# Last layer's second quantised product: Pool rounds the lower four channel blocks, VectorE the upper four

## The chip, the cores and the metric

The kernel runs on one core of one Trainium2 chip. The time is the device time of the whole program in microseconds (us), median of the runs. The core's engines are TensorE (PE in the profile, its weight loads PEld), VectorE (DVE), ScalarE (ACT), GpSimd (POOL, here called Pool) and SyncE (SP). They run side by side, each works through its own queue in order, and they meet only at semaphores: an instruction that waits holds back everything behind it on its engine.

## The reference, cut to what matters

The input is x of shape (4, 1024, 256). Four layers follow one another, each an attention over a context of 77 rows and a feed-forward part. The change is in the feed-forward part of the last layer:

```python
def act_quant(x):
    scale = 127.0 / jnp.clip(jnp.max(jnp.abs(x), axis=-1, keepdims=True), 1e-05)
    return jnp.clip(jnp.round(x * scale), -128, 127) / scale
def weight_quant(w):
    scale = 1.0 / jnp.clip(jnp.mean(jnp.abs(w)), 1e-05)
    return jnp.clip(jnp.round(w * scale), -1, 1) / scale
def bit_linear(x, w):
    return jnp.einsum('bsd,hd->bsh', act_quant(x), weight_quant(w))  # straight-through term left out
h = bit_linear(x, w1)                      # 256 -> 1024 channels
h = depthwise_conv1d(h, conv_w, conv_b)    # width 3, along the tokens
h = jax.nn.silu(h)
return bit_linear(h, w2)                   # 1024 -> 256 channels
```

For the second product each token has its own scale, 127 over the largest absolute value among its 1024 channels. So no value can be scaled and rounded before all 1024 channels of that token are there.

## The kernel before, in words

`layer_3` (from L2377) works on one batch b of 1024 tokens after another, four in all (B = 4). A batch is two groups g of 512 tokens (G = 2, TOK = 512), a group four tiles of 128 tokens (TT = 4). Each batch has an attention part of eight units (`attention_dve`, `attention_act`, `attention_pool`, `attention_pe`), in which VectorE subtracts the row maximum from the scores, ScalarE takes the exponential, VectorE sums, Pool multiplies by the reciprocal sum (L286), and TensorE transposes and multiplies; after it the first product, the convolution and SiLU.

The hidden values of a batch lie in SBUF as `SL`, 128 partitions x 8 channel blocks (NHC = 8, HALF = 4) x 1024 tokens in f32, channels on the partitions. TensorE turns each block (L2586), VectorE takes the maxima (L2747). When all eight are done, VectorE works out 127 / maximum (L2753 to L2757), TensorE spreads it over the partitions (L2632), and ScalarE copies it to SBUF as `S2B` (L2542; the tile bears the name L3PT in the profile). Then comes what is called the tail here, four VectorE instructions for each group, each over 4 blocks x 512 tokens, that is 128 x 2048 elements:

- L2762 multiplies the lower four blocks of `SL` by the scale, in place; both of its inputs are in SBUF.
- L2763 does so for the upper four, and is linked: VectorE waits for its end.
- L2764 rounds the lower four into `SQ` (bf16), by adding and subtracting a large constant (MAGIC); one input, in SBUF.
- L2765 rounds the upper four, and raises `q_ready[g]`.

The order is group 0 entirely, then group 1. `second_product` (L2559 on, its products are L2566) waits for `q_ready[g]` and runs 32 products of 128 x 256, the eight blocks of one token tile after another. For batches 0 to 2 it is called within the attention of the next batch: TensorE's queue has the scores of unit 0 and of unit 1 for both groups ahead of `second_product(0)`, those of unit 2 ahead of `second_product(1)`. For the last batch both stand at the end of the program, followed by `add_output` on VectorE (L2697) and the stores. On VectorE the next batch's attention stands directly behind the tail; its first instructions are L245 (maximum over scores in PSUM) and L246 (subtraction, one input in PSUM, one in SBUF). On Pool, whose queue in this layer holds the attention's L286, the bias L2467 and the next batch's keys and values (`last_layer_context`, L2084 and L2086), nothing stands between those keys and values and the first L286 of the next batch.

Of the kernel before, what the change touches and what calls it, by code (L numbers as in the profile page):

```python
# [10 lines left out]
ALU = mybir.AluOpType  # L11
# [10 lines left out]
G = 2  # L22
TT = 4
TOK = TT * P
# [10 lines left out]
MAGIC = 12582912.0  # L35
# [111 lines left out]
def bc_last(ap, n):  # L147

    return ap.unsqueeze(len(ap.shape)).to_broadcast(list(ap.shape) + [n])


def bc_at(ap, axis, n):
    v = ap.unsqueeze(axis)
    shape = list(v.shape)
    shape[axis] = n
    return v.to_broadcast(shape)
# [1924 lines left out]
def last_layer_context(eng, L, headof, blockhead):  # L2081

    for c in range(KC):
        eng.tensor_tensor(L["Kbd"][c][:, :, :], bc_at(L["ctxT3"][:, c, :], 1, HH), bc_last(headof[:, :], CTXP), ALU.mult)  # L2084
    for j in range(BLK):
        last = eng.tensor_tensor(L["Vbd"][j][:, :, :].rearrange("p c (h d) -> p c h d", d=DH),  # L2086
                                 L["ctxrows"][:, j, :].rearrange("p (c h d) -> p c h d", c=KC, d=DH),
                                 bc_at(bc_last(blockhead[:, j, :], DH), 1, KC), ALU.mult)
    return last
# [287 lines left out]
def layer_3(L, nc, a, sbt, GP, SC, ident, identb, onesf, headof, blockhead, eps, tokno, spare, x1rows, buf, out):  # L2377
    ctx = ExitStack()
    BT = G * TT
    HALF = NHC // 2  # L2380
    with ctx:
        def sb(name, shape, dt=f32):
            return sbt(name, shape, dt, ctx)
# [18 lines left out]
        SL = sb("SL", [P, NHC, S])  # L2402
        SQ = sb("SQ", [P, NHC, S], bf16)

        S2B = T["PT"][1][:, :, :, :].rearrange("p a b c -> p (a b c)")[:, 0:S]
# [8 lines left out]
        with rnd:  # L2414
            sa = Sems(nc, rnd)
            sm = {n: sa.pair("l3_" + n) for n in ATTENTION_SEMS + (
                "x_in", "x_out", "var1_ready", "sd1_ready", "rstd1_ready", "xn1_ready",
                "var2_ready", "sd2_ready", "rstd2_ready", "xn2_ready", "xt_psum", "xt_ready",
                "y_psum", "y_taken", "xqt_psum", "sx_ready", "xr_ready", "xq_ready", "xq_high", "xq_low", "h_psum", "z0_ready", "z_ready", "s_ready",
                "am_ready", "tile_psum", "tile_taken", "s2_psum", "s2_ready", "q_ready", "o_psum", "o_ready",  # L2420
                "x_bias")}
            vchain, ctx_in, kv_ready = (sa.one("l3_" + n) for n in ("vchain", "ctx_in", "kv_ready"))

            with nc.Block() as block:
# [35 lines left out]
                @block.gpsimd  # L2460
                def _(pool):
                    for b in range(B):
                        def after_unit(v):
                            if v < G:
                                x = X[b % 2][v][:, :, :]
                                pool.wait_ge(sm["xn1_ready"][v], b + 1)
                                nc.gpsimd.tensor_tensor(x, x, bc_at(bo3r[:, :], 1, TT), ALU.add).then_inc(sm["x_bias"][v], 1)  # L2467
                        attention_pool(nc, pool, T, sm, b, after_unit)
                        if b + 1 < B:
                            for g in range(G):  # L2470
                                pool.wait_ge(sm["ot_psum"][g], UNITS * (b + 1))
                            pool.wait_ge(ctx_in, CTX_IN * (b + 1))
                            last_layer_context(nc.gpsimd, L, headof, blockhead).then_inc(kv_ready, 1)

                @block.scalar
                def _(act):
# [71 lines left out]
                def _(pe):  # L2548
# [12 lines left out]

                    def second_product(g, b):
                        pe.wait_ge(sm["q_ready"][g], b + 1)
                        for t in range(TT):
                            for h in range(NHC):
                                last = nc.tensor.matmul(GP[g][:, t * D:(t + 1) * D], SQ[:, h, (g * TT + t) * P:(g * TT + t + 1) * P], w2q[:, h, :],  # L2566
                                                        start=h == 0, stop=h == NHC - 1)
                        last.then_inc(sm["o_psum"][g], 1)
# [73 lines left out]
                def _(dve):  # L2642
                    link = Chain(dve, vchain)
                    tt, tsc, stt = nc.vector.tensor_tensor, nc.vector.tensor_scalar, nc.vector.scalar_tensor_tensor
# [62 lines left out]
                    for b in range(B):  # L2707
                        def after_slot(slot):
                            if b and 0 < slot <= G:
                                add_output(slot - 1, b - 1)  # L2710
                        attention_dve(nc, dve, T, sm, b, link, SC, after_slot)
                        for g in range(G):
                            add_projection(g, b, 0)
                        for g in range(G):
                            add_projection(g, b, 1)
                        for g in range(G):
                            ln_rstd(g, b, 2)
                        if b + 1 < B:
                            tokens_stats(0, b + 1)
                        for g in range(G):  # L2720
                            quantise(g, b)
                        if b + 1 < B:
                            tokens_stats(1, b + 1)
                        for g in range(G):
                            dve.wait_ge(sm["xr_ready"][g], b + 1)
                            for t in range(TT):
                                xn = T["XN"][g][:, t, :]
                                last = tsc(xn, xn, MAGIC, isx[g][:, t:t + 1], ALU.subtract, ALU.mult)
                            last.then_inc(sm["xq_ready"][g], 1)
                        if b + 1 < B:  # L2730
                            for g in range(G):
                                ln_rstd(g, b + 1, 1)
                        for g in range(G):
                            dve.wait_ge(sm["xq_high"][g], b + 1)
                            hi, lo = (v[:, :, :].rearrange("p k n -> p (k n)") for v in XQ[g])
                            tt(lo, GP[g][:, :], hi.bitcast(f32), ALU.subtract).then_inc(sm["xq_low"][g], 1)

                        for h in range(NHC + 2):
                            if h < NHC:
                                z, y = Z[h % 2], SC[h % 2]  # L2740
                                dve.wait_ge(sm["z0_ready"][h % 2], b * HALF + h // 2 + 1)
                                link(stt(z[:, 1:S], y[:, 0:S - 1], cwc[:, h, 0:1], z[:, 1:S], ALU.mult, ALU.add))  # L2742
                                stt(z[:, 0:S - 1], y[:, 1:S], cwc[:, h, 2:3], z[:, 0:S - 1], ALU.mult, ALU.add).then_inc(sm["z_ready"][h % 2], 1)  # L2743
                            if h >= 2:
                                i = h - 2
                                dve.wait_ge(sm["tile_psum"][i % 2], b * HALF + i // 2 + 1)
                                nc.vector.tensor_reduce(amh[:, :, i], GP[i % 2][:, :].rearrange("p (t n) -> p t n", n=P), AX, ALU.max,  # L2747
                                                        apply_absolute_value=True).then_inc(sm["tile_taken"][i % 2], 1)
                        for i in range(2):
                            dve.wait_ge(sm["tile_taken"][i], (b + 1) * HALF)  # L2750
                        for g in range(G):
                            s = slice(g * TT, (g + 1) * TT)
                            link(nc.vector.reduce_max(am2[:, s], amh[:, s, :], AX))  # L2753
                            link(tsc(am2[:, s], am2[:, s], 1e-5, None, ALU.max))
                            link(nc.vector.reciprocal(s2[:, s], am2[:, s]))
                            tsc(s2[:, s], s2[:, s], 127.0, None, ALU.mult).then_inc(sm["am_ready"][g], 1)
                            link(tsc(os2[:, s], am2[:, s], 1.0 / 127.0, wm2[:, :], ALU.mult, ALU.mult))  # L2757
                        for g in range(G):
                            tok = slice(g * TOK, (g + 1) * TOK)
                            low, high, by = SL[:, 0:HALF, tok], SL[:, HALF:, tok], bc_at(S2B[:, tok], 1, HALF)  # L2760
                            dve.wait_ge(sm["s2_ready"][g], b + 1)
                            tt(low, low, by, ALU.mult)  # L2762
                            link(tt(high, high, by, ALU.mult))  # L2763
                            tsc(SQ[:, 0:HALF, tok], low, MAGIC, MAGIC, ALU.add, ALU.subtract)  # L2764
                            tsc(SQ[:, HALF:, tok], high, MAGIC, MAGIC, ALU.add, ALU.subtract).then_inc(sm["q_ready"][g], 1)  # L2765
                    for g in range(G):
                        add_output(g, B - 1)
# [51 lines left out]
```

## Time and profile before

| | us |
|---|---|
| median of 3 runs | 2816.32 (2815.0 to 2820.91) |
| the profiled execution | 2818.34 |
| its span, first to last instruction | 2816.6 |
| PE / DVE / ACT / POOL busy in the span | 2333.1 / 1941.5 / 1471.4 / 1035.7 |
| layer 3's four tails, first L2762 of each | starts at 2407.03, 2536.86, 2666.64, 2793.21 |

Busy time is summed over the whole program, so it doesn't say what a stage waits for. The timeline gives, in order of time, the instructions of each engine with their start, the time they took (equal neighbours are merged, with their count), and in brackets how long the engine had been idle before and what ended that. The chain of waits follows the work that ended last back through what released it. The granted clock (PEclk) is TensorE's clock as a share of 2.4 GHz: 0.50 is the lower level, 1.2 GHz, and 1.00 the upper.

### The profile page before, as it was taken

To read this page: it belongs to the slowest core of one execution; us is meant where nothing else is said; L and a number is where in the kernel's file an instruction comes from. 1 tells how busy PE (TensorE), PEld (TensorE's weight loads), DVE (VectorE), ACT (ScalarE), POOL (GpSimd) and SP (SyncE) were. 2 spreads that over 40 slices of the span, in tenths; PEclk is the share of its full clock that TensorE was granted. 3 is DMA by queue.
4 is the path that set the end of the run, shared out by engine and by line. 5 is a ranking of instruction groups with operands and counts; after the bars stand their busy time and mean duration, and the time that the engine had idled before them with its cause. 6 is when DMAs were issued, how large, how long until landed. Compare 5 with 4: busy or idle time off the path is not lost. (4 is left out here: it accounts for less than half of the span.)

```text
span 2816.6 us, 43303 instructions
## 1 busy us (share of the span) xinstructions
PE 2333.1 (83%) x16184; PEld 1911.5 (68%) x16184; DVE 1941.5 (69%) x4456; ACT 1471.4 (52%) x2446; POOL 1035.7 (37%) x1011
## 2 busy tenths in 40 slices
PE   4778888877589999999975999999999956767575
PEld 2445455554377888888865999999999935445444
DVE  4698888895355666666654666676666647978877
ACT  2457777664355565565452544444455435454543
POOL 3243444432132344443453444454444432213030
PEclk9789988886789999999987999999999978888887
DMA  8600000000100001100014555555555320001000
GB/s 266 229 1 17 4 14 16 8 9 8 33 16 1 26 28 44 48 31 21 17 50 142 112 126 141 137 116 134 141 133 130 65 52 11 31 11 31 0 16 15
DMA packets 144472, 171.03 MB, mean 61 GB/s; under 512 B 16920, under 2 KB 114053, under 8 KB 144264
## 3 DMA queue, kind: packets, MB, share of 16 engines
q1 hardware_dynamic: 114360, 136.15, 14.7%
q0 software_dynamic: 29184, 31.99, 7.8%
q8 instruction: 129, 2.11, 0.3%
q14 instruction: 79, 0.65, 0.1%
q10 hardware_dynamic: 720, 0.12, 0.0%
HBM read 100.73 MB, written 74.32 MB: 62 GB/s over the span
## 5 line engine op out<-in xcount | busy, mean ns | idle before, releaser
L2191 POOL DMA_INDIRECT x_after_l<-rowsout,target x160 | 266.6, 1666 | 319.6 <-DVE rowsout L2317 261.5
L162 PE MATMUL SC<-Xhi,Whi 128*128 128x320 f32 x1024 | 321.7, 314 | 6.6 <-DVE HF L2359 3.6
L162 PE MATMUL SC<-Xhi,Wlo 128*128 128x320 f32 x1024 | 317.5, 310 | 0.0
L162 PE MATMUL SC<-Xlo,Whi 128*128 128x320 f32 x1024 | 317.3, 310 | 0.0
L645 POOL TENSOR_TENSOR PR<-PR,rs 128x616 f32<-128x616 f32 x128 | 163.2, 1275 | 390.4 <-DVE rs L1039 390.4
L1406 POOL TENSOR_TENSOR ff_Hlo<-ff_HF,ff_Hhi 128x512 fp32r<-128x512 f32 x108 | 143.2, 1326 | 387.8 <-ACT ff_Hhi L1539 387.8
L2288 ACT ACTIVATE SG<-SC 128x320 f32<-128x320 f32 x256 | 111.9, 437 | 237.3 <-PE SC L162 235.9
L2324 DVE TENSOR_TENSOR Hlo<-HF,Hhi 128x320 fp32r<-128x320 f32 x256 | 129.7, 507 | 104.3 <-ACT Hhi L2276 104.3
L162 PEld LDWEIGHTS SC<-Xhi,Whi 128*128 128x128 f32 x1024 | 193.4, 189 | 10.1 <-DVE HF L2359 7.2
L1808 DVE TENSOR_TENSOR ff_HF<-ff_HG,SC 128x512 f32<-128x512 f32 x112 | 76.7, 685 | 172.6 <-ACT ff_HG L1533 112.9
L162 PEld LDWEIGHTS SC<-Xlo,Whi 128*128 128x128 f32 x1024 | 193.5, 189 | 0.0
L162 PEld LDWEIGHTS SC<-Xhi,Wlo 128*128 128x128 f32 x1024 | 193.2, 189 | 0.0
L286 POOL TENSOR_TENSOR L3PR<-L3PR,L3rs 128x616 f32<-128x616 f32 x64 | 76.9, 1226 | 315.4 <-DVE L3rs L253 315.2
L2276 ACT ACTIVATE Hhi<-HF 128x320 fp32r<-128x320 f32 x256 | 120.7, 472 | 130.9 <-DVE HF L2359 130.8
L162 PE MATMUL GP<-Whi,Hhi 128*128 128x256 f32 x640 | 182.6, 285 | 4.9 <-DVE Hlo L2324 2.8
L162 PE MATMUL GP<-Wlo,Hhi 128*128 128x256 f32 x640 | 182.5, 285 | 0.0
L162 PE MATMUL GP<-Whi,Hlo 128*128 128x256 f32 x640 | 182.3, 285 | 0.0
L181 PE MATMUL SC<-Kbd,QT 64*128 64x308 f32 x512 | 120.5, 552 | 52.7 <-DVE PR L1033 48.8
L744 ACT ACTIVATE PT<-GP 128x640 f32<-128x640 f32 x128 | 89.6, 700 | 116.4 <-PE GP L895 115.9
L2359 DVE TENSOR_TENSOR HF<-SG,SC 128x320 f32<-128x320 f32 x256 | 124.1, 485 | 34.2 <-ACT SG L2288 32.7
L895 PE MATMUL GP<-ident,PR 128*128 128x128 f32 x640 | 111.9, 314 | 42.5 <-ACT OT L740 25.8
L1419 POOL DMA_INDIRECT expert_in<-raw,ff_slot_in x128 | 127.7, 998 | 50.3 <-issue 33.5
(498 smaller groups left out, 6874.4 us busy)
## 6 DMA issues: line engine op xcount, KB each, us to landing
expert_in<-zeros SPq DMA_DIRECT2D x4, 5440.0 KB, 35.7
rowsin<-expert_in SPq DMA_DIRECT2D x32, 680.0 KB, 4.5
first_expert<-L_wg SPq DMA_DIRECT2D x16, 512.0 KB, 5.4
first_expert<-L_wu SPq DMA_DIRECT2D x16, 512.0 KB, 6.4
first_expert<-L_wd SPq DMA_DIRECT2D x16, 512.0 KB, 7.4
Wraw<-L_wg SPq DMA_DIRECT2D x16, 512.0 KB, 5.5
Wraw<-L_wu SPq DMA_DIRECT2D x16, 512.0 KB, 6.4
Wraw<-L_wd SPq DMA_DIRECT2D x16, 512.0 KB, 7.3
```

The costliest lines, as they stand in the source:

```text
L162: last = nc.tensor.matmul(out, lhs[l], rhs[r], start=start and n == 0, stop=stop and n == 2)
L181: last = nc.tensor.matmul(o[j], q[r], K[r, 4 * j:4 * j + 4, 0:CTX], start=mask is None, stop=True)
L645: nc.gpsimd.tensor_tensor(pr, pr, bc_last(rs[n % NPA][:, :], CTX), mult).then_inc(pnorm, 1)
L744: nc.scalar.activation(PT[:, n % 2, :, :], ptrans[:, 0:BLK * P].rearrange("p (k n) -> p k n", n=P), ACT.Copy).then_inc(pt_ready, 1)
L895: last = nc.tensor.transpose(ptrans[:, k * P:(k + 1) * P], pr[:, k * P:(k + 1) * P], ident[:, :])
L1406: nc.gpsimd.tensor_tensor(lo[:, :], HF[q % 2][:, :], hi[:, :].bitcast(f32), ALU.subtract).then_inc(h_low, 1)
L1419: nc.gpsimd.indirect_dma_start(buf[:, :], bass.IndirectOffsetOnAxis(ap=slot_in[g][:, t, k:k + 1], axis=0), T["XS"][g][:, t, :], None, boun ...
L2191: nc.gpsimd.indirect_dma_start(x1rows[:, :], bass.IndirectOffsetOnAxis(ap=target[j % 2][:, t:t + 1], axis=0), rowsout[j % 2][:, t, :], Non ...
L2276: nc.scalar.activation(Hsp[q // NU % 2][0][:, h, n * CC:(n + 1) * CC], HF[q % 2][:, :], ACT.Copy).then_inc(h_high, 1)
L2288: nc.scalar.activation(SG[u % 2][:, :], SC[u % 2][:, 0:CC], ACT.Silu).then_inc(s_ready, 1)
L2324: nc.vector.tensor_tensor(lo_, HF[q % 2][:, :], hi_.bitcast(f32), ALU.subtract).then_inc(h_made, 1)
L2359: nc.vector.tensor_tensor(HF[u % 2][:, :], SG[u % 2][:, :], SC[u % 2][:, 512:512 + CC], ALU.mult).then_inc(h_mult, 1)
```

## The change

Pool takes over the rounding of the lower four blocks (128 x 2048, f32 to bf16) for both groups. VectorE multiplies the lower blocks of both groups first, each raising a new semaphore `scaled[g]`; then it multiplies and rounds the upper blocks group by group. Pool raises `low_rounded[g]`, and `second_product` waits for it beside `q_ready[g]`. Pool's two instructions stand behind the next batch's keys and values in its queue.

```diff
@@ gpsimd, end of each batch
                             last_layer_context(nc.gpsimd, L, headof, blockhead).then_inc(kv_ready, 1)
+                        for g in range(G):
+                            tok = slice(g * TOK, (g + 1) * TOK)
+                            pool.wait_ge(sm["scaled"][g], b + 1)
+                            nc.gpsimd.tensor_scalar(SQ[:, 0:HALF, tok], SL[:, 0:HALF, tok], MAGIC, MAGIC, ALU.add, ALU.subtract)\
+                                .then_inc(sm["low_rounded"][g], 1)
@@ tensor
                     def second_product(g, b):
                         pe.wait_ge(sm["q_ready"][g], b + 1)
+                        pe.wait_ge(sm["low_rounded"][g], b + 1)
@@ vector, the tail
                         for g in range(G):
                             tok = slice(g * TOK, (g + 1) * TOK)
-                            low, high, by = SL[:, 0:HALF, tok], SL[:, HALF:, tok], bc_at(S2B[:, tok], 1, HALF)
+                            low = SL[:, 0:HALF, tok]
                             dve.wait_ge(sm["s2_ready"][g], b + 1)
-                            tt(low, low, by, ALU.mult)
-                            link(tt(high, high, by, ALU.mult))
-                            tsc(SQ[:, 0:HALF, tok], low, MAGIC, MAGIC, ALU.add, ALU.subtract)
+                            tt(low, low, bc_at(S2B[:, tok], 1, HALF), ALU.mult).then_inc(sm["scaled"][g], 1)
+                        for g in range(G):
+                            tok = slice(g * TOK, (g + 1) * TOK)
+                            high = SL[:, HALF:, tok]
+                            link(tt(high, high, bc_at(S2B[:, tok], 1, HALF), ALU.mult))
                             tsc(SQ[:, HALF:, tok], high, MAGIC, MAGIC, ALU.add, ALU.subtract).then_inc(sm["q_ready"][g], 1)
```

## Rows read from the trace of the kernel before

**Rows 1.** Chain of waits, 2400 to 2432 us (start, us, what).
```profile
2406.33 0.60 ACT L3PT L2542
...
2420.72 0.72 DVE L3mx L245
...
2422.32 0.70 PE SC L178 x2
```
**Rows 2.** Timeline around the first tail (start, us, engine, line, operation, idle before).
```profile
2407.03 2.29 DVE L2762 TENSOR_TENSOR SL<-SL,L3PT 128x2048 f32<-128x2048 f32 x1 [0.80 <-ACT L3PT L2542]
...
2420.64 0.79 DVE L245 TENSOR_REDUCE L3mx<-SC 128x8 f32<-128x616 f32 x1
...
2426.25 3.71 PE L2566 MATMUL GP<-w2q,SQ 128*128 128x256 bf16 x32
...
2429.01 2.40 POOL L286 TENSOR_TENSOR L3PR<-L3PR,L3rs 128x616 f32<-128x616 f32 x2 [75.62 <-DVE L3rs L253]
```
**Rows 3.** Timeline of DVE alone, the last tail.
```profile
2793.21 2.29 DVE L2762 TENSOR_TENSOR SL<-SL,L3PT 128x2048 f32<-128x2048 f32 x1 [0.80 <-ACT L3PT L2542]
2795.42 2.28 DVE L2763 TENSOR_TENSOR SL<-SL,L3PT 128x2048 f32<-128x2048 f32 x1
2797.74 1.23 DVE L2764 TENSOR_SCALAR SQ<-SL 128x2048 bf16<-128x2048 f32 x1
2798.88 1.22 DVE L2765 TENSOR_SCALAR SQ<-SL 128x2048 bf16<-128x2048 f32 x1
2800.01 2.28 DVE L2762 TENSOR_TENSOR SL<-SL,L3PT 128x2048 f32<-128x2048 f32 x1
...
2804.53 1.23 DVE L2764 TENSOR_SCALAR SQ<-SL 128x2048 bf16<-128x2048 f32 x1
2805.68 1.22 DVE L2765 TENSOR_SCALAR SQ<-SL 128x2048 bf16<-128x2048 f32 x1
2806.81 1.65 DVE L2697 SCALAR_TENSOR_TENSOR X<-GP,os,X 128x256 f32<-128x256 f32 x4
```
**Rows 4.** Timeline of PE alone, the last second products.
```profile
2800.15 6.14 PE L2566 MATMUL GP<-w2q,SQ 128*128 128x256 bf16 x32 [6.71 <-DVE SQ L2765]
2806.95 3.67 PE L2566 MATMUL GP<-w2q,SQ 128*128 128x256 bf16 x32 [0.65 <-DVE SQ L2765]
```
**Rows 5.** Busy time by window (window, length, PE to POOL busy, PEclk, DMA).
```profile
2800.10:2803.00 2.90, 2.85 (x14) 2.04 (x15) 2.90 (x2) 0.00 (x0) 0.00 (x0) 0.50 0.00 0
```
**Rows 6.** Timelines of DVE and of POOL, one DVE instruction without and with Pool.
```profile
870.82 0.48 DVE L1869 TENSOR_TENSOR ff_PR<-ff_PR,ff_rs 128x308 f32<-128x308 f32 x1
...
953.21 1.47 DVE L1869 TENSOR_TENSOR ff_PR<-ff_PR,ff_rs 128x308 f32<-128x308 f32 x1
...
953.05 1.29 POOL L1406 TENSOR_TENSOR ff_Hlo<-ff_HF,ff_Hhi 128x512 fp32r<-128x512 f32 x1 [5.70 <-ACT ff_Hhi L1539]
```
**Rows 7.** Timelines of DVE and of POOL, 1087.0 to 1089.8 us.
```profile
1087.13 1.23 DVE L1969 TENSOR_TENSOR ff_XTlo<-ff_XT,ff_XThi 128x1024 fp32r<-128x1024 f32 x1 [0.20 <-ACT ff_XThi L1485]
...
1087.63 1.87 POOL L1406 TENSOR_TENSOR ff_Hlo<-ff_HF,ff_Hhi 128x512 fp32r<-128x512 f32 x1 [0.70 <-ACT ff_Hhi L1539]
```
**Rows 8.** Timelines of DVE and of POOL, two DVE instructions back to back.
```profile
1521.26 2.36 DVE L2302 TENSOR_TENSOR Wlo<-first_expert,Whi 128x1024 fp32r<-128x1024 f32 x2 [13.20 <-ACT Whi L2264]
...
2080.47 2.37 DVE L2302 TENSOR_TENSOR Wlo<-Wraw,Whi 128x1024 fp32r<-128x1024 f32 x2 [0.46 <-ACT Whi L2264]
...
2080.56 1.19 POOL L2180 TENSOR_TENSOR mine<-mine 128x10 f32<-128x10 f32 x1
```
**Rows 9.** Groups of Pool's instructions, whole span (count, busy us, mean ns, idle before).
```profile
L2180 POOL TENSOR_TENSOR mine<-mine 128x10 f32<-128x10 f32 x32 | 8.3, 260 | 2.5
L485 POOL TENSOR_SCALAR_AFFINE_SELECT spread<-spread 80x640 f32<-80x640 f32 x8 | 6.0, 747 | 1.1
L1425 POOL TENSOR_TENSOR ff_wd_lo<-raw,ff_wd_hi 128x2560 fp32r<-128x2560 f32 x1 | 5.6, 5640 | 31.1 <-ACT ff_wd_hi L1543 31.1
...
L485 POOL TENSOR_SCALAR_AFFINE_SELECT ident<-ident 128x128 f32<-128x128 f32 x1 | 0.3, 287 | 0.2 <-POOL spread L490 0.2
```

More of the change, by code:

```diff
@@ L2419, in layer_3 @@
                 "y_psum", "y_taken", "xqt_psum", "sx_ready", "xr_ready", "xq_ready", "xq_high", "xq_low", "h_psum", "z0_ready", "z_ready", "s_ready",
-                "am_ready", "tile_psum", "tile_taken", "s2_psum", "s2_ready", "q_ready", "o_psum", "o_ready",
+                "am_ready", "scaled", "low_rounded", "tile_psum", "tile_taken", "s2_psum", "s2_ready", "q_ready", "o_psum", "o_ready",
                 "x_bias")}
```

## The prediction

> **What bounds the kernel now.** I read the chain of waits first, around a tail in the middle of the layer. ScalarE's copy of the scale ends it from the one side, then VectorE's eight tail instructions follow without a break, then the next batch's first maximum L245, and only then TensorE's next scores, L178 [rows 1]. So in batches 0 to 2 the tail is on the path whole: from the start of L2762 at 2407.03 to the start of L245 at 2420.64 are 13.61 us [rows 2], and the reader is to see that L245 has no idle time before it. What the tail loses or gains, the next attention starts sooner or later. Two things have slack there. The second product of group 0 starts only at 2426.25, 19.2 us after the tail began, and Pool's next own work at 2429.01, after 75.62 us of idleness [rows 2].
>
> The last batch is another case, since nothing follows but the second products. The timeline of VectorE gives the steps from one start to the next [rows 3]: L2762 to L2763 2.21 us, L2763 to L2764 2.32 (the link costs 0.1), L2764 to L2765 1.14, L2765 to the next 1.13; together 13.60 for both groups. Group 0's `q_ready` comes 6.9 us after the tail's start, and TensorE begins at 2800.15, at a granted clock of 0.50, the level of 1.2 GHz [rows 4, 5], after 6.71 us of idleness. Its 32 products take 6.14 us. Group 1's begin at 2806.95, 13.74 after the tail's start, and take 3.67 [rows 4]. Between the two TensorE is idle for 0.65. That number decides much below: only 0.65 us can group 0 come later before the end moves.
>
> **The change part by part.** Counted from the start of a tail, with no disturbance by Pool, VectorE's queue after the change would be: L2762 for group 0 at 0, for group 1 at 2.21, upper product of group 0 at 4.42, its rounding at 6.74, upper product of group 1 at 7.88, its rounding at 10.20, next work at 11.33. Removed are two roundings, 2 x 1.14 = 2.28 us. Group 0's `q_ready` would be at 6.74 + 1.22 = 7.96, so 1.07 later than before, because it now has three products ahead of it and not two.
>
> Pool gets two roundings of 128 x 2048. The trace has no large one-input Pool instruction with a bf16 result. The nearest is L485, one input: 747 ns for 640 elements, 287 for 128 [rows 9], so 0.90 ns an element, and 287 + 1920 x 0.90 = 2.01 us for 2048. The other end is Pool with two full inputs, L1425: 5640 ns for 2560 elements, 2.20 ns each, so 4.5 us. Nothing speaks for a rounding below 2.0. I take 2.01, since the instruction has one input, and keep 4.5 for the range.
>
> Now whether Pool's work lies beside VectorE's. A VectorE product of two SBUF tiles, L1869, takes 0.48 us alone; where Pool's L1406 had begun 0.16 earlier it takes 1.47 [rows 6]. So it did not share, it stood still 0.99 us, to 0.14 before Pool's record ends. The other direction: L1406, 1.29 us in [rows 6], takes 1.87 where it begins 0.50 after VectorE's L1969, another product of two SBUF tiles [rows 7]. Its end at 1089.50 lies 1.14 after L1969's end; it did next to nothing in between. These are exclusive turns. All of VectorE's multiplications in the tail have two SBUF inputs. Pool's rounding reads SBUF as L1406 does. I expect that nothing overlaps: each of Pool's roundings takes its 2.01 - 0.14 = 1.87 us out of VectorE's time, where it falls between VectorE's SBUF instructions. The rounding on VectorE, 1.14 us a step for 2048 elements, nearly two elements in a ns, is the form that I expect to be excluded too, though that is argued from the two-input rows.
>
> The Trainium skill, page "SBUF — State Buffer", section "Who interferes with whom", says the same of both kinds: VectorE with two SBUF inputs, or in a two-port mode, and a GpSimd instruction that reads SBUF take the shared ports for a whole instruction in turn, and whoever comes second stands still. Rows 6 and 7 agree for two inputs, with 0.99 us and 0.58 us; by this rule the forecast below stands, and without it the second rival does. Its page "GPSIMD Engine Reference", section "Engine selection", calls one-input work on GpSimd roughly line rate, which with its 1.2 GHz would be an estimate of 1.7 us for 2048 elements, 0.3 under my term; the sum would be some 2 us smaller.
>
> Next, who goes first. `scaled[0]` comes at 2.29, when the second L2762 has begun (2.21). Pool stands waiting until that ends at 4.42. Does Pool get in there, though VectorE's next instruction is queued without a gap? One place shows it: Pool's L2180 began 0.09 us after the first of two back-to-back L2302, and ended at 2081.75, just behind the first (half of the pair's 2.37 lies at 2081.66) and far ahead of the second's end at 2082.84 [rows 8]. It took 1.19 where it has a mean of 0.26 [rows 9]. The VectorE pair took 2.37 in place of 2.36 [rows 8], so it gave way only as long as those 10 elements need. Whoever waits comes next. So Pool rounds group 0 at 4.42 to 6.3, ahead of the upper product of group 0. Whether its second rounding follows at once or after that product makes no difference: in both orders it is ahead of the rounding of the upper blocks of group 0.
>
> The middle batches: 11.33 + 2 x 1.87 = 15.07 in place of 13.60, that is 1.47 later each, and three of them 4.4 us. `low_rounded[0]` comes by 6.5 and `low_rounded[1]` by 10.6, far ahead of TensorE's 19.2, so the new wait on TensorE costs nothing; behind it stand the scores of unit 2. If that cover were gone, each us would hold back TensorE, and with it those scores. Pool's own attention work is not moved, it has 8 us between L245 and L286 [rows 2].
>
> The last batch: `q_ready[0]` at 7.96 + 3.74 = 11.70, 4.8 later than before. TensorE starts at 11.75 cold as before and needs 6.14, to 17.89; `q_ready[1]` at 15.2 is earlier than that, so group 1 follows at once, to 21.56. Before it ended at 13.74 + 3.67 = 17.41. That is 4.15 us later, which is more than the VectorE time, since TensorE's slow product is now the path. The last add and the stores follow unchanged.
>
> The sum is 4.4 + 4.15 = 8.5 us more. Of the profiled execution's 2818.34 that makes 2826.9; the median of the runs is 2.02 lower, 2816.32, and I predict it as 2824.8. Within this case the turns may fall otherwise: if Pool's second rounding were to come only after group 0's upper rounding, group 0 would be ready 1.87 sooner and the sum 6.7. With 0.3 us more or less for a rounding it moves by 4 tails x 2 x 0.3 = 2.4. The likeliest case has its own range at 2822 to 2828.
>
> **The rivals.**
>
> First, the same turns with a slow Pool. At 4.5 us a rounding, 4.36 of it in VectorE's way, a middle tail is 11.33 + 8.72 = 20.05, 6.45 more, three 19.4. The last has `q_ready[0]` at 16.68, TensorE's end at 16.7 + 6.14 + 3.67 = 26.5, 9.1 later. Sum 28.5, 2844.8. For it speaks the conversion to bf16 with two operations in one instruction, which L485 doesn't show. Against it, that L1425's price is that of two inputs.
>
> Second, on the other side: no exclusion, because Pool's one-input reading and VectorE's products do lie beside each other. Then each middle tail gains 2.28, three 6.8. In the last TensorE starts at 8.0 and ends at 8.0 + 6.14 + 3.67 = 17.8, 0.4 later than before. Sum -6.4, 2809.9. The point from which a middle tail gains is at 1.14 us of VectorE's time for each of Pool's roundings, half of the 2.28 removed. Against it stand rows 6 and 7; for it, that both show Pool with two inputs.
>
> Third, Pool finds no gap and gets through only behind VectorE's last rounding, at 11.33. The middle tails gain 2.28 each all the same, as L245 and L246 read PSUM and TensorE's 19.2 is not reached by 15.3. In the last, `low_rounded[0]` comes at 13.3, TensorE ends at 13.4 + 6.14 + 3.67 = 23.2, 5.8 later. Sum -6.8 + 5.8 = -1.0, 2815.3. Against it stands the one place in rows 8, for it that this is one place only, with 10 elements.
>
> **How the numbers follow.** A measurement of this kernel can tell a difference of about 0.2%, 5.6 us. The forecast has a chance of 0.55, the slow Pool 0.15, no exclusion 0.10, Pool behind VectorE 0.15, and 0.05 are for what I don't see. The range goes from 2813 to 2844: below are most of the second rival and a part of the unseen, above nearly half of the first. Faster by over 0.2% is the second rival in its better half and little else, 0.08. Within 0.2% are the third, the rest of the second, and 0.05 of the forecast with a quicker Pool, 0.24. Slower is what remains, 0.68.
>
> **What would show it.** In the changed kernel's timeline the middle tail from the first L2762 to the next L245 should be near 15.1 us. One or two VectorE instructions of the tail should show durations of 4 us or so in place of 2.28 or 1.22, each ending where a Pool rounding ends plus its own length. Pool's first rounding should begin at 2.4 and seem long, since it stands waiting from there to 4.4. Group 0's last products should begin near 11.8 us. The prediction is wrong if the six VectorE instructions that are left in a tail keep their durations (then the second or third rival, told apart by Pool's durations), or if the middle tails are above 17 us (the first).

## The result and the profile after

The changed kernel takes 2843.82 us (median of 4 runs, 2842.74 to 2845.12), the kernel before 2816.68 beside it: ratio 1.0097, 95% interval 1.0083 to 1.0111, 27.1 us slower. The forecast was 8.5 us slower. Direction and place were right, the size is off by a factor of three, and the time stands near the price of the first rival (28.5 us slower).

The first middle tail after the change, timelines of VectorE and of Pool (start, us, engine, line, operation, idle before); it answers to [rows 2, 3].

```profile
2404.93 4.49 DVE L2768 TENSOR_TENSOR SL<-SL,L3PT 128x2048 f32<-128x2048 f32 x2 [0.81 <-ACT L3PT L2547]
2409.34 6.60 DVE L2772 TENSOR_TENSOR SL<-SL,L3PT 128x2048 f32<-128x2048 f32 x1
2415.98 1.50 DVE L2773 TENSOR_SCALAR SQ<-SL 128x2048 bf16<-128x2048 f32 x1
2417.40 6.57 DVE L2772 TENSOR_TENSOR SL<-SL,L3PT 128x2048 f32<-128x2048 f32 x1
2424.01 1.49 DVE L2773 TENSOR_SCALAR SQ<-SL 128x2048 bf16<-128x2048 f32 x1
2425.42 0.78 DVE L245 TENSOR_REDUCE L3mx<-SC 128x8 f32<-128x616 f32 x1
...
2407.31 9.09 POOL L2477 TENSOR_SCALAR SQ<-SL 128x2048 bf16<-128x2048 f32 x1 [56.02 <-DVE SL L2768]
2416.39 8.03 POOL L2477 TENSOR_SCALAR SQ<-SL 128x2048 bf16<-128x2048 f32 x1
```

The reader is to see three things. The tail takes 2425.42 - 2404.93 = 20.49 us in place of 13.61. Both lower products keep their length, 4.49 for two; each upper product takes 6.6 in place of 2.28, that is 4.3 more, and each upper rounding 1.5 in place of 1.22. And Pool's two roundings are recorded from 2407.31 to 2424.42 without a gap, with waiting in both: the first stands until the second lower product ends at 2409.42, and the second, 8.03 us long, begins while VectorE's rounding of group 0 (2415.98 to 2417.48) is still going on.

The last second products, timeline of TensorE, which answers to [rows 4]:

```profile
2824.02 5.04 PE L2572 MATMUL GP<-w2q,SQ 128*128 128x256 bf16 x32 [12.34 <-DVE SQ L2773]
2832.04 3.67 PE L2572 MATMUL GP<-w2q,SQ 128*128 128x256 bf16 x32 [2.98 <-DVE SQ L2773]
```

The last tail starts at 2811.45, so group 1's products start 20.59 us behind it, where it was 13.74. The loss adds up from four equal parts: from the first to the last tail the changed kernel takes 2811.45 - 2404.93 = 406.52 us, before 386.18, so 20.3 for three tails; in the last one 6.85. That is 27.2. Where TensorE's slow product was to be the path in the last batch, it is not: it is idle for 2.98 us between the groups.

### The profile page after: what moved, and what is told of

The parts are those of the page before. It is cut to its first block and busy times, and to the rows that moved or that the text cites. A ratio compares the mean times of both kernels' runs of the same rounds, so it can differ in the third digit from the quotient of the medians.

```text
span 2841.7 us, 43311 instructions
## 1 busy us (share of the span) xinstructions
PE 2329.0 (82%) x16184; PEld 1910.0 (67%) x16184; DVE 1969.2 (69%) x4448; ACT 1471.1 (52%) x2446; POOL 1103.9 (39%) x1019
## 5 line engine op out<-in xcount | busy, mean ns | idle before, releaser
L2477 POOL TENSOR_SCALAR SQ<-SL 128x2048 bf16<-128x2048 f32 x8 | 68.3, 8551 | 235.1 <-DVE SL L2768 235.1
```

## The experiments

### Is Pool slow by itself, or are both slowed by being together?

The first theory, T: Pool's rounding is simply long, and VectorE waits for a part of it. The rival, R: Pool alone needs the 2.0 us of the forecast, and the two slow each other.

```diff
                             high = SL[:, HALF:, tok]
+                            for i in range(G):
+                                dve.wait_ge(sm["low_rounded"][i], b + 1)
                             link(tt(high, high, bc_at(S2B[:, tok], 1, HALF), ALU.mult))
```

> VectorE waits for both of Pool's roundings before the upper products, so that Pool and VectorE never read SBUF side by side after the lower products. In the changed kernel Pool's first rounding ended 6.98 us after the second lower product; take away the 2.28 us of VectorE's product that lay in it and 4.70 are left. Theory T (turns, and Pool is slow by itself): alone Pool still needs about 4.7 us a rounding, VectorE's L2772 and L2773 fall back to 2.28 and 1.22, and a middle tail is 4.5 + 2 x 4.7 + 6.9 = 20.8 us, where the changed kernel has 20.5; the time is 2844 to 2850. Rival R (each slows the other, Pool alone would be the 2.0 us of the forecast): Pool 2.0 a rounding, tail 4.5 + 4.0 + 6.9 = 15.4 us, 5.1 less each, time near 2825.

Measured: 2862.78 us, ratio to before 1.0158 (1.0141 to 1.0175), above the range of either. The timelines of Pool and of VectorE in this run:

```profile
2410.47 16.15 POOL L2477 TENSOR_SCALAR SQ<-SL 128x2048 bf16<-128x2048 f32 x2 [56.02 <-DVE SL L2768]
...
2426.73 2.29 DVE L2774 TENSOR_TENSOR SL<-SL,L3PT 128x2048 f32<-128x2048 f32 x1 [14.14 <-POOL SQ L2477]
2429.06 1.23 DVE L2775 TENSOR_SCALAR SQ<-SL 128x2048 bf16<-128x2048 f32 x1
```

With Pool alone, VectorE's instructions are back at 2.29 and 1.23. But Pool is not at 4.7: from the end of the second lower product (2412.58) to Pool's end (2426.62) are 14.0 us, 7.0 a rounding. The view of the line (minimum, median, maximum in ns) has the second rounding, which waits for nothing, as the minimum:

```profile
L2477 POOL TENSOR_SCALAR SQ<-SL x8: 7075/8066/9095, 2410.5 to 2837.3; 128x2048 bf16<-128x2048 f32 x8
```

R is refuted. T is right in kind and wrong in number: I had subtracted VectorE's 2.28 us from Pool's 6.98, as if they had excluded each other. They had overlapped, which is why this kernel, where they can't, is 19 us slower still than the changed one.

### What a Pool instruction costs by its form

Eight Pool instructions were added to the kernel before, each once in each of the batches 0 to 2. Shown are only they, with remarks; the scratch tiles are left out (`src` and `dstb` have rows of 512, `fsrc`, `fdstb` and `fdst` are contiguous, a `b` at the end means bf16).

```diff
+plink(nc.gpsimd.tensor_scalar(dstb, src, MAGIC, MAGIC, ALU.add, ALU.subtract))     # rows of 512, bf16
+plink(nc.gpsimd.tensor_scalar(fdstb, fsrc, MAGIC, MAGIC, ALU.add, ALU.subtract))   # contiguous, bf16
+plink(nc.gpsimd.tensor_scalar(fdst, fsrc, MAGIC, MAGIC, ALU.add, ALU.subtract))    # contiguous, f32
+plink(nc.gpsimd.tensor_scalar(fdstb, fsrc, MAGIC, None, ALU.add))
+plink(nc.gpsimd.tensor_scalar(fdst, fsrc, MAGIC, None, ALU.add))
+plink(nc.gpsimd.tensor_tensor(fdst, fsrc, fsrc, ALU.mult))
+plink(nc.gpsimd.tensor_copy(fdst, fsrc))
+plink(nc.gpsimd.tensor_scalar(fdstb[:, 0:TOK], fsrc[:, 0:TOK], MAGIC, MAGIC, ALU.add, ALU.subtract))
```

> The kernel before, with eight more Pool instructions per batch in Pool's idle stretch before the tail, each 128 x 2048 (the last 128 x 512) on scratch tiles, one after the other: the changed kernel's form (four rows of 512, f32 to bf16, add and subtract), the same contiguous, the same with f32 output, with one operation and bf16, with one operation and f32, a product of two inputs, a copy, and the first form on 512 elements. It leaves nothing out. Theory T: the first form takes 4.7 to 4.9 us with nobody beside it. Rival R: 2.0 us. If T, the rows say what costs: bf16 output, the second operation, or the rows; I expect the second operation and the conversion to share the 2.7 us above 2.0, contiguity nothing. The time should be that of before, Pool having slack there.

Measured: 2900.42 us, one execution. The timeline of Pool in this run, eight forms in the order of the diff:

```profile
2507.71 7.09 POOL L2480 TENSOR_SCALAR pc<-pa 128x2048 bf16<-128x2048 f32 x1
2514.88 7.09 POOL L2481 TENSOR_SCALAR pc<-pa 128x2048 bf16<-128x2048 f32 x1
2522.05 7.08 POOL L2482 TENSOR_SCALAR pb<-pa 128x2048 f32<-128x2048 f32 x1
2529.22 5.37 POOL L2483 TENSOR_SCALAR pc<-pa 128x2048 bf16<-128x2048 f32 x1
2534.67 5.36 POOL L2484 TENSOR_SCALAR pb<-pa 128x2048 f32<-128x2048 f32 x1
2540.11 3.60 POOL L2485 TENSOR_TENSOR pb<-pa 128x2048 f32<-128x2048 f32 x1
2543.78 1.89 POOL L2486 COPY pb<-pa 128x2048 f32<-128x2048 f32 x1
2545.76 2.01 POOL L2487 TENSOR_SCALAR pc<-pa 128x512 bf16<-128x512 f32 x1
```

Rows and bf16 cost nothing, though I had given the conversion a share. The second operation costs 1.72 us. The form itself costs most: with one operation it takes 5.36, nearly three times the copy's 1.89, and more than a product (3.60, here of a tile with itself). From 512 to 2048 elements it rises by 5.08, 3.3 ns an element. So a one-input Pool instruction can be slower than a two-input one, and my upper end of 4.5 us was no upper end.

The trace of before had a better hint, in rows I had passed over. Groups of Pool's instructions in the kernel before, the same form on small tiles with one operation (count, busy us, mean ns):

```profile
L2178 POOL TENSOR_SCALAR mine<-rowsin 128x20 f32<-128x20 f32 x32 | 9.3, 292 | 73.0 <-DMA x_after_l<-rowsout,target 69.4 <-DMA rowsin<-expert_in 3.6
...
L2182 POOL TENSOR_SCALAR empty<-rowsin 128x5 f32<-128x5 f32 x32 | 7.8, 243 | 2.8
```

49 ns for 15 elements are 3.3 ns each, which for 2048 makes 6.9 us. These rows have one operation, for which it is too much (5.4), so that it comes near the 7.1 of two operations is in part luck; L485, which I took, is another operation and gave 2.0.

I had expected the time of before, since Pool is idle in this stretch. It was 83 us more, because VectorE was delayed there, as is told below.

### Held, or served in turn?

How can VectorE's product lose 4.3 us beside an instruction of 7.1, and both end within 0.5 us of each other? The run with the forms has an instruction that tells it, a VectorE one of 4 elements with two SBUF inputs, begun 0.08 us behind Pool's first form. Timelines of VectorE and of Pool:

```profile
2350.29 4.45 DVE L2691 SCALAR_TENSOR_TENSOR L3nw<-L3nw,L3rstd 128x4 f32<-128x4 f32 x1
2354.78 0.16 DVE L2692 SCALAR_TENSOR_TENSOR L3rstd<-L3nw,L3rstd 128x4 f32<-128x4 f32 x1
...
2350.21 7.12 POOL L2480 TENSOR_SCALAR pc<-pa 128x2048 bf16<-128x2048 f32 x1
```

It stood still for 4.3 us, the next of the same kind took 0.16 again, though Pool's instruction went on until 2357.33. So VectorE and Pool meet not only at semaphores, but also where both read SBUF. To see the same in the tail, the upper product was cut in two.

```diff
-                            link(tt(high, high, bc_at(S2B[:, tok], 1, HALF), ALU.mult))
+                            for k in range(2):
+                                part = high[:, k * 2:(k + 1) * 2, :]
+                                last = tt(part, part, bc_at(S2B[:, tok], 1, 2), ALU.mult)
+                            link(last)
```

> The upper product of each group is cut in two of 128 x 1024, with no wait between them. Two readings of the 6.57 us that an upper product takes beside Pool's 7.08 us rounding. Held (theory H): VectorE stands still for about 4.3 us, as L2691 on 4 elements did in the run with Pool's forms (4.45 us in place of 0.16), and then runs at full speed beside the rest of Pool's instruction: first half 4.3 + 1.2 = 5.5 us, second half 1.2. Paced (rival P): both instructions get an element in turn, 3.2 ns each: two halves of about 3.3 us. The time is 2844 in both.

Measured: 2843.43 us, 1.0094 (1.0076 to 1.0113). The two halves of the first upper product in VectorE's timeline, and the view of the line:

```profile
2409.77 5.54 DVE L2774 TENSOR_TENSOR SL<-SL,L3PT 128x1024 f32<-128x1024 f32 x1
2415.23 1.21 DVE L2774 TENSOR_TENSOR SL<-SL,L3PT 128x1024 f32<-128x1024 f32 x1
...
L2774 DVE TENSOR_TENSOR SL<-SL,L3PT x16: 1209/3356/5539, 2409.8 to 2829.8; 128x1024 f32<-128x1024 f32 x16
```

The first half takes 5.54 and the second 1.21, in group 1 likewise 5.50 and 1.21. The median of 3356 ns lies halfway between the two kinds and is no instruction's own length. Held it is: VectorE stands for 4.3 us, then runs at full speed beside the rest of Pool's instruction. Why Pool lets go of reading there is not shown.

### Is it the second SBUF input?

The changed kernel, with the scale read from PSUM. The diff is cut to what matters; VectorE waits for TensorE (`s2_psum`) where it waited for ScalarE's copy.

```diff
-                            tt(low, low, bc_at(S2B[:, tok], 1, HALF), ALU.mult)
+                            tt(low, low, bc_at(SC[g][:, 0:TOK], 1, HALF), ALU.mult)
-                            link(tt(high, high, bc_at(S2B[:, tok], 1, HALF), ALU.mult))
+                            link(tt(high, high, bc_at(SC[g][:, 0:TOK], 1, HALF), ALU.mult))
-                            nc.scalar.activation(S2B[...], SC[g][:, 0:TOK], ACT.Copy)
+                                pe.wait_ge(sm["q_ready"][g], b)     # ahead of the next batch's first scores
```

> The scale is read by VectorE from PSUM, where TensorE wrote it, so that the four products of a tail have only one SBUF input; ScalarE's copy (0.60 us) falls away, and the next batch's scores wait for q_ready. Theory T with the exclusion tied to VectorE's second SBUF input: all products keep about 2.3 us though Pool is at work beside them; only L2773-like roundings still wait for Pool. The tail is between 12 us (one short wait) and 17 us (both Pool roundings ahead of the first upper rounding), the time 2810 to 2828. Rival R (whatever reads SBUF on VectorE is slowed by Pool): products stay near 6.6 us, tail near 20 us, time about 2840.

Measured: 2830.39 us, 1.0044 (1.0027 to 1.0060), a little above the range given. Timelines of VectorE and Pool:

```profile
2409.38 2.28 DVE L2771 TENSOR_TENSOR SL<-SL,SC 128x2048 f32<-128x2048 f32 x1
2411.70 3.87 DVE L2772 TENSOR_SCALAR SQ<-SL 128x2048 bf16<-128x2048 f32 x1
2415.48 2.27 DVE L2771 TENSOR_TENSOR SL<-SL,SC 128x2048 f32<-128x2048 f32 x1
2417.79 5.79 DVE L2772 TENSOR_SCALAR SQ<-SL 128x2048 bf16<-128x2048 f32 x1
2423.50 0.78 DVE L245 TENSOR_REDUCE L3mx<-SC 128x8 f32<-128x616 f32 x1
...
2407.36 15.14 POOL L2477 TENSOR_SCALAR SQ<-SL 128x2048 bf16<-128x2048 f32 x2 [55.39 <-DVE SL L2767]
```

The products are at 2.28 with Pool at work beside them: it is the second SBUF input that makes them wait. Now the roundings wait. The second ends at 2423.58, 1.08 behind Pool's end at 2422.50, so it did nothing until Pool was through. That is the other kind of conflict: VectorE's rounding, nearly two elements in a ns, stands until the end of Pool's instruction. The first one shows it best: it begins at 2411.70, 4.34 us after Pool's, about when a product would have been let go, and ends only at 2415.57. The tail is 18.5 us and not 12 to 17, because Pool's instruction was longer than I then believed.

It also explains the 83 us of the run with the forms, most of them at least: its first tail starts 24.8 us later than that of before, and the next two stretches from tail to tail are 28.9 and 27.9 longer. VectorE's small one-input instructions ahead of the feed-forward part's first product are of this second kind. L2702, L2704 and L2742 take 28.2 us there in the first batch, in the kernel before 2.8. L2704, 4 elements, took 6.92 us and ended with Pool's instruction:

```profile
2364.77 6.92 DVE L2704 TENSOR_SCALAR sx<-sx 128x4 f32<-128x4 f32 x1
...
2364.59 7.08 POOL L2482 TENSOR_SCALAR pb<-pa 128x2048 f32<-128x2048 f32 x1
```

The Trainium skill, page "SBUF — State Buffer", section "Summary: rules for kernel authors", has both kinds, and says that the second one to issue stands until the first is through. For the fast rounding the runs agree. For two SBUF inputs they differ: 4.3 us of 7.1.

### The order alone

VectorE does all four roundings again, in the changed kernel's order; Pool's part and its semaphores, taken out, are not shown.

```diff
                             link(tt(high, high, bc_at(S2B[:, tok], 1, HALF), ALU.mult))
+                            tsc(SQ[:, 0:HALF, tok], SL[:, 0:HALF, tok], MAGIC, MAGIC, ALU.add, ALU.subtract)
                             tsc(SQ[:, HALF:, tok], high, MAGIC, MAGIC, ALU.add, ALU.subtract)
```

> The changed kernel's order on VectorE (both lower products first) with all four roundings on VectorE and none on Pool. T: middle tails 13.6 us as before; in the last batch group 0 is ready 2.2 us later, of which 0.65 were slack, so 1.5 us in all, about 2818. If the order itself carried a part of the 27 us loss, it would show here as more than 3 us.

Measured: 2816.61 us, 0.9997 (0.9988 to 1.0007). So the order carries at most 2.0 of the 27.1 us. The 1.5 us expected would lie within the interval; the timeline shows that they didn't come. The last products of this run, all 64 in one row of TensorE's timeline:

```profile
2799.12 8.61 PE L2566 MATMUL GP<-w2q,SQ 128*128 128x256 bf16 x64 [8.91 <-DVE SQ L2768]
```

They start 9.14 us behind the tail's start, as worked out, but end 17.75 behind it, only 0.34 later than before. My 6.14 us for group 0 hung on where in them the granted clock rose and was no property of the work: before, it stood at 0.50 for 4.9 us from their start; in the changed kernel, where the same 32 products took 5.04, it was at 1.00 again 3 us after it.

### The forecast's own case: a short Pool instruction

```diff
-                            nc.gpsimd.tensor_scalar(SQ[:, 0:HALF, tok], SL[:, 0:HALF, tok], MAGIC, MAGIC, ALU.add, ALU.subtract)
+                            nc.gpsimd.tensor_copy(SQ[:, 0:HALF, tok], SL[:, 0:HALF, tok])
```

> Pool copies the lower blocks to bf16 in place of rounding them (the rounding of these blocks is left out; all orders and waits stay). Pool's copy alone took 1.89 us where the rounding takes 7.08, so this is the forecast's case, with the size that the forecast had assumed. By the forecast's sum with 1.89 - 0.14 = 1.75 in VectorE's way: middle tail 11.33 + 3.5 = 14.8 us, 1.2 more than before, three 3.7; last batch 3.5 to 4 us more; 2824 in all. If the loss of the changed kernel came from something else than the length of Pool's instruction, the time stays above 2835.

Measured: 2830.67 us, 1.0047 (1.0031 to 1.0062). Timelines of VectorE and Pool:

```profile
2407.13 4.49 DVE L2768 TENSOR_TENSOR SL<-SL,L3PT 128x2048 f32<-128x2048 f32 x2 [0.80 <-ACT L3PT L2547]
2411.54 3.98 DVE L2772 TENSOR_TENSOR SL<-SL,L3PT 128x2048 f32<-128x2048 f32 x1
2415.55 2.80 DVE L2773 TENSOR_SCALAR SQ<-SL 128x2048 bf16<-128x2048 f32 x1
2418.27 2.27 DVE L2772 TENSOR_TENSOR SL<-SL,L3PT 128x2048 f32<-128x2048 f32 x1
...
2421.72 0.79 DVE L245 TENSOR_REDUCE L3mx<-SC 128x8 f32<-128x616 f32 x1
...
2409.49 7.78 POOL L2477 CAST SQ<-SL 128x2048 bf16<-128x2048 f32 x2 [56.00 <-DVE SL L2768]
```

The tail is 14.59 us, the forecast's way of adding gives 14.8. The turns are as described: Pool gets in between two queued products, VectorE loses 1.70 and 1.58. (Both Pool records contain waiting, and the copy to bf16 was not measured alone; the 1.89 is that of a copy to f32.) But the time is 6.7 us above what I expected. From one tail to the next it is 133.22 us, 3.4 more than before, with only 1.0 of it in the tail. The other 2.4 lie behind it, at the attention's start. The windows of that stretch, each counted from L245's start, first this kernel, then the kernel before (window, length, busy PE to POOL, PEclk):

```profile
2427.10:2431.10 4.00, 4.00 (x27) 2.94 (x26) 3.38 (x7) 1.45 (x2) 1.00 (x1) 0.68 0.00 0
...
2441.10:2446.10 5.00, 4.99 (x52) 3.05 (x50) 2.03 (x3) 2.90 (x5) 1.50 (x1) 0.78 0.88 277
```

```profile
2426.00:2430.00 4.00, 4.00 (x36) 3.26 (x34) 3.40 (x7) 1.45 (x2) 0.98 (x1) 0.95 0.02 4
...
2440.00:2445.00 5.00, 4.95 (x60) 2.88 (x56) 4.37 (x7) 3.63 (x8) 0.76 (x2) 1.00 0.85 251
```

The granted clock is 0.68 where it was 0.95, and 0.78 later where it was 1.00. In the first stretch lies the second product of group 0, 4.77 us in place of 3.71, in the other ten transposes, 2.37 in place of 1.28. The forecast had no term for it.

The last batch, TensorE's timeline:

```profile
2814.64 9.15 PE L2572 MATMUL GP<-w2q,SQ 128*128 128x256 bf16 x64 [11.04 <-DVE SQ L2773]
```

All 64 products follow one another without a gap and end 20.43 us behind the tail's start, 3.0 later than before.

### Pool behind VectorE

The changed kernel, with Pool's two roundings waiting for VectorE's last one.

```diff
-                            pool.wait_ge(sm["scaled"][g], b + 1)
+                            pool.wait_ge(sm["q_ready"][1], b + 1)
```

> The changed kernel, but Pool's two roundings wait for VectorE's last one (q_ready of group 1), so that no VectorE instruction with two SBUF inputs or of the fast form lies beside them. Held reads and Pool's length being the cause: VectorE's tail is 11.3 us, 2.3 less than before. But Pool's 2 x 7.08 us now end 25.5 us after the tail's start, so TensorE's first second product waits 1.6 us and the attention's first L286 some 6 us: each middle stretch 1 to 3 us longer than before. In the last batch TensorE waits for Pool until 18.5 and 25.6: 29.3 in place of 17.4, 12 us more. Time 2830 to 2838. If Pool's rounding were harmless to VectorE, this run would differ from the changed kernel only by Pool's lateness and be slower than 2844.

Measured: 2834.72 us, 1.0065 (1.0049 to 1.0080), inside the range. VectorE's tail is 11.33 us, exactly the uncontended queue of the forecast; Pool is late instead: TensorE's first product waits 1.76 us for it, and L286 starts only at 2431.88, when Pool is free. In the last batch the products end 12.0 us later than before, but the three middle stretches are only 0.3, 2.9 and 2.1 us longer. So it beats the changed kernel by 9 us: between batches Pool's length costs less where nothing of VectorE's is held.

### ScalarE in Pool's place, and the clock

ScalarE adds the constant in place and subtracts it into bf16. In the last batch VectorE goes group by group. The diff is cut to ScalarE's part.

```diff
+nc.scalar.activation(low, low, ACT.Identity, bias=magic[:, :]).then_inc(sm["low_up"][g], 1)
+act.wait_ge(sm["low_up"][g], b + 1)
+nc.scalar.activation(SQ[:, 0:HALF, g * TOK:(g + 1) * TOK], low, ACT.Identity, bias=nmagic[:, :]).then_inc(sm["low_rounded"][g], 1)
```

> ScalarE rounds the lower blocks, in two passes (adding the constant in place, then subtracting it into bf16), Pool does nothing there; in the last batch VectorE goes group by group. If the loss is Pool's length and its hold on VectorE's reads, ScalarE's roundings disturb nothing: products 2.28, roundings 1.22, middle tails 11.3 us (2.3 less than before, three 6.8), the last batch about 1.3 us shorter; ScalarE's passes about 1.95 us each, 7.8 for both groups, done at about 12 us, before the exponential that waits for them in its queue has its input (12.9 us). Time 2808 to 2811. If VectorE is slowed by any engine that reads SBUF beside it, tails stay above 13 us and the time at 2817 or more.

Measured: 2813.44 us, 0.9984 (0.9975 to 0.9993): faster than before by 0.16%, less than expected. VectorE's timeline and ScalarE's:

```profile
2409.31 2.29 DVE L2778 TENSOR_TENSOR SL<-SL,L3PT 128x2048 f32<-128x2048 f32 x1
2411.64 1.23 DVE L2779 TENSOR_SCALAR SQ<-SL 128x2048 bf16<-128x2048 f32 x1
...
2416.24 0.79 DVE L245 TENSOR_REDUCE L3mx<-SC 128x8 f32<-128x616 f32 x1
...
2408.87 1.99 ACT L2507 ACTIVATE SL<-SL,magic 128x2048 f32<-128x2048 f32 x1
2410.89 2.00 ACT L2509 ACTIVATE SQ<-SL,nmagic 128x2048 bf16<-128x2048 f32 x1
```

ScalarE disturbs VectorE in nothing; the tail is 11.34 us. Yet the stretches from tail to tail are 129.98, 125.86 and 126.88 us, where before has 129.83, 129.78 and 126.57: only the second has the gain. To test the clock as the cause, TensorE got products that nobody reads.

```diff
+def keep_warm(n):
+    for i in range(n):
+        nc.tensor.matmul(GP[1][:, 512:1024], identb[:, :], w2q[:, 0:2, :].rearrange("p h n -> p (h n)"), start=True, stop=True)
+keep_warm(24)     # behind the first scores of batches 1 to 3; 22 ahead of the last second products
```

> e6_act_last with idle products on TensorE (24 of 128 x 512 behind the first scores of a batch, 22 ahead of the last second products), whose results nobody reads, so that TensorE is not idle during VectorE's tail. If TensorE's clock at the seam is what swallowed e6's gain: the granted clock is 1.00 where the attention starts, its four score products take 0.79 us in place of 1.40 and the first second product 3.67 in place of 4.78, each stretch from tail to tail is 3.5 to 5 us shorter than e6's longest, the last products take 3.67 each; 2795 to 2802 in all. If the clock is not it, the time is e6's 2813 or more, as the idle products can only delay.

Measured: 2805.26 us, 0.9958 (0.9945 to 0.9972), the fastest of all, 12 us under before, but 3 above the range. Its timeline of TensorE:

```profile
2412.08 5.35 PE L2601 MATMUL GP<-w2q,identb 128*128 128x512 bf16 x24
...
2420.16 0.79 PE L181 MATMUL SC<-Kbd,L3XT 64*128 64x308 f32 x4
...
2422.42 3.67 PE L2576 MATMUL GP<-w2q,SQ 128*128 128x256 bf16 x32
```

The granted clock is 1.00 from 2416.2 to 2426, where it was 0.50 and then 0.68 without the idle products: four score products take 0.79 us (1.40 without), the second product 3.67 (4.78). The stretches are 126.25, 126.25 and 123.06, each 3.5 or 3.6 shorter than before. The 22 idle products in the last batch gave nothing in this execution: the clock fell once more behind group 0, group 1 took 5.32, and the products end 17.49 us behind the tail's start, where they ended at 16.33 without.

Reading the scale from PSUM was tried in the kernel before by itself, with ScalarE's rounding, and with this and the idle products. The edits are those shown above.

> The kernel before, with VectorE reading the scale from PSUM, where TensorE wrote it; ScalarE's copy (0.60 us and a semaphore) is gone, and the next batch's scores wait for q_ready. VectorE's products take 2.28 from either place, as in the run with the scale from PSUM. Each tail starts 0.65 us earlier, 2.6 in all: 2814. If the scores that now wait for q_ready are late, it is nothing: the first maximum would show idle time.

Measured: 2815.34 us, 0.9993 (0.9984 to 1.0002), no difference that can be told. The shorter start is there (the tail starts 0.17 us behind TensorE's spreading of the scale, with no copy between), but the scores of group 1, which now wait for `q_ready`, are late: group 1's first maximum waits 0.59 us for them, where before it waited for nothing.

> ScalarE's rounding as in e6_act_last, and the scale read from PSUM as in e8_before_psum. If the two gains add, e6's 3.7 us and e8's 1.8 us make 2811.6. The loss behind the tail that e6 showed (its tail was 2.27 us shorter, but the first and third stretch from tail to tail were 0.14 and 0.31 us longer) is put down to TensorE's clock: the third maximum of the attention is late, since 2nd products and scores ran longer at 1.2 GHz. If that is so, the same stretch may again swallow the gain of some batches, by 2.4 us each.

Measured: 2806.58 us, 0.9963 (0.9949 to 0.9976), 5 us better than the sum of the two. The stretches are 126.48, 126.34 and 124.77. Here the granted clock rose ahead of the second product, which took 3.67 us in the first batch and not 4.78; I had not foreseen it, and why it rose sooner is not shown.

> e7_act_psum with the idle products of e12_act_warm. All three together: 0.65 us a tail under e12, so 2793 to 2800. The scores wait for q_ready, so the idle products stand behind that wait and start only when group 1 is ready; if they then run past the point where VectorE needs scores, this run is slower than e12.

Measured: 2815.73 us, 0.9994 (0.9985 to 1.0003), 16 us above the range. The warning in the expectation came true: the idle products start only behind the last `q_ready`, and VectorE waits for them. Timeline of VectorE:

```profile
2428.84 0.80 DVE L245 TENSOR_REDUCE L3mx<-SC 128x8 f32<-128x616 f32 x1 [6.15 <-PE SC L181]
```

## Why the prediction was wrong

- **What bounds the kernel**: right. A tail grew by 6.9 us, and all but 0.1 of it arrived in the time in each of the four batches.
- **The step that failed**: "I take 2.01, since the instruction has one input". It is 7.08 us alone. The number of inputs is not what sets Pool's time for this form, and the slope of another operation (L485) was carried to it. The upper end of 4.5 was too low for the same reason. The first rival came within 1.4 us of the measured loss by luck, from two errors that cancel: a rounding too short by 2.6 us, and all of it but 0.14 in VectorE's way. The 1.7 us that the prediction worked out from the Trainium skill, page "GPSIMD Engine Reference", section "Engine selection", by which one-input work is roughly at line rate, is further off still: of the forms measured only the copy, 1.89 us, is near it.
- **"Exclusive turns"**: half right. Short Pool products exclude VectorE nearly whole, as [rows 6, 7] show, and so does the copy (1.70 and 1.58 us); this long form holds a product with two SBUF inputs for 4.3 us of 7.1, and the fast rounding for its full length. That the fast form is excluded too was argued only, and is shown now.
- **Who goes first**: right for Pool's first rounding. With the rounding and with the copy alike Pool got in between two queued products, so the third rival is out; the second is out by the 6.6 us. Its second was to come ahead of group 0's upper rounding "in both orders". With the copy it did (2.80 us for that rounding), in the changed kernel it came behind: VectorE's rounding took only 1.50, Pool's next waited for it, and group 0 was ready at 12.57. The prediction had this order as a side case.
- **The middle batches**: the queue without Pool was right to 0.01 us (11.33, measured in the run with Pool behind VectorE). The term of 3.74 us for Pool's turns was 9.16. With the short copy the way of adding held, 14.8 against 14.59.
- **The last batch**: the term of 4.15 us was 6.85, and by another mechanism. Group 1 was late by VectorE's own queue, with Pool's holds in it; TensorE's first 32 products were not the path. With the short copy they were, and the loss was 3.0, since the clock rose sooner in them than the 6.14 us had it.
- **Missing**: TensorE's clock behind the tail. It made no difference in the changed kernel, where the second product took 3.67 us (3.71 before), but it went with 2.4 us a middle batch with the copy, so that even with the right length the sum of 8.5 would have been short of the 13.5 measured there.

## What to carry to other kernels

Price an offloaded instruction by a row of the same form on the same engine, even if it is a tiny one: here the price from two small tiles was some 30% too high for its own form, that from another operation too low by a factor of 3.5 for the form that was used. Look then at what the neighbour engine does meanwhile; ScalarE took the same work at 4.0 us a group and held nobody. And where a stage ends with TensorE idle, expect a gain or loss of one or two us there to be changed by what the clock does next.

## What the runs showed of the hardware

- Pool's one-input instruction with a constant takes 5.36 us for 2048 elements, 7.08 with two operations, against 3.60 for a product and 1.89 for a copy.
- A Pool instruction of this form holds VectorE's two-input instructions for 4.3 us and its fast one-input ones for all 7.1, and it does so to a VectorE instruction of 4 elements too (4.45 and 6.92 us). A VectorE product with its second input in PSUM is not held (2.28 us).
- 32 equal products on TensorE took 3.67, 4.78, 5.04, 5.32, 6.14 and 6.57 us, by where in them the granted clock rose or fell. 5.4 us of products that nobody reads, in TensorE's idle time of each middle tail, made the kernel 0.3% faster (2813.44 to 2805.26); behind a late semaphore they cost it back (2815.73, against 2806.58 without them).
